# adaLN attention + ternary FFN block on one core: the reciprocal rms is spread through DRAM, and the input is scaled in the next step's layer norm stretch

## What is computed

```python
xn  = rms_norm(x, g_norm) * (1.0 + scale) + shift        # scale, shift: cond @ W_emb + b_emb, one row per sequence
q, k, v = split(xn @ W_qkv);  q, k = rms_norm(q), rms_norm(k)
o   = softmax(q @ k.T * d**-0.5) @ v;  y = o + o @ W_out
h   = gelu(bitlinear(y, w_fc));  x = x + bitlinear(h, w_proj)   # bitlinear: layer_norm, absmax quant, ternary weights
rms_norm(x, g) = x * rsqrt(mean(x * x) + 1e-6) * g
```

## Time and profile before

| what | us |
|---|---|
| median of 3 runs | 1168.1 (1166.49 to 1168.19) |
| profiled execution, its own time | 1165.45 |
| its span, first to last instruction | 1163.6 |
| PE busy / DVE busy / ACT busy / POOL busy | 1075.8 / 895.6 / 814.5 / 543.1 |
| length of a step in the loop, from one `cur_s` (L1151) to the next | 65.95 |
| start of step 0, 1, 2 by the same instruction | 48.76, 122.32, 193.06 |

### The profile page before, as it was taken

The page is one execution under the profiler, slowest core; times in us unless marked ns, Lnnn a source line. Parts: engine busy times, 40 slices in busy tenths (PEclk is TensorE's granted clock), DMA queues, the critical chain, the costliest instruction groups (busy, mean ns, idle before and its releaser), DMA issues.

```text
span 1163.6 us, 26244 instructions
## 1 busy us (share of the span) xinstructions
PE 1075.8 (92%) x9484; PEld 675.8 (58%) x9484; DVE 895.6 (77%) x1616; ACT 814.5 (70%) x1372; POOL 543.1 (47%) x365
## 2 busy tenths in 40 slices
PE   5646899999999999999999999999999999999797
PEld 1324565666666565666666565666666566666463
DVE  4668768888788888878787888878787888877544
ACT  4866575867768586877768586876868586775752
POOL 1522173643718173553718174463808264462425
PEclk8868899999999999999999999999999999999889
DMA  9810303112130313112031212112131212002101
GB/s 341 302 28 1 92 20 74 56 36 57 38 90 36 72 54 72 54 25 66 36 90 36 72 54 54 55 33 75 36 90 36 72 54 45 29 25 50 38 1 55
DMA packets 75501, 74.20 MB, mean 64 GB/s; under 512 B 6592, under 2 KB 56000, under 8 KB 74944
## 3 DMA queue, kind: packets, MB, share of 16 engines
q1 hardware_dynamic: 75456, 73.59, 21.7%
HBM read 39.89 MB, written 8.39 MB: 41 GB/s over the span
## 4 chain that ended last, share of the span: by engine, by line
PE 74%; DVE 11%; ACT 9%; issue 3%; DMA 1%; SPq 0%; DVEq 0%; ACTq 0%; POOL 0%
PE F L625 10%; PE F L627 10%; PE F L782 5%; PE F L783 5%; PE QA L593 3%; PE QA L594 3%; PE QA L595 3%; PE QB L593 3%; PE QB L594 3%; PE QB L595 3%; DVE rowmax L1088 2%; PE T L813 2%; PE SA L681 2%; DVE xn_lo L1075 2%; PE SB L681 2%
## 5 line engine op out<-in xcount | busy, mean ns | idle before, releaser
L552 POOL TENSOR_TENSOR rqk<-ssq,half 128x16 f32<-128x16 f32 x64 | 186.8, 2920 | 93.6 <-DVE ssq L1241 93.4
L782 PE MATMUL F<-yT_hi,fc_t 128*128 128x256 f16 x1024 | 227.7, 274 | 0.0
L783 PE MATMUL F<-yT_lo,fc_t 128*128 128x256 f16 x1024 | 227.3, 273 | 0.0
L625 PE MATMUL F<-proj_t,hs 128*128 128x512 f16 x512 | 196.6, 384 | 3.8 <-DVE hs L1206 3.8
L627 PE MATMUL F<-proj_t,hs 128*128 128x512 f16 x512 | 196.1, 383 | 0.0
L1206 DVE SCALAR_TENSOR_TENSOR hs<-hg,g_inv,hs 128x512 f16<-128x512 f32 x128 | 142.3, 1112 | 46.4 <-ACT hs L922 44.5
L520 POOL TENSOR_TENSOR acc<-acc,hg 128x512 f32<-128x512 f32 x96 | 148.0, 1542 | 8.6
L527 POOL TENSOR_TENSOR acc<-acc,hq 128x512 f32<-128x512 f32 x96 | 123.1, 1282 | 18.4 <-ACT hq L978 8.1
L917 ACT ACTIVATE hg<-F,g_fc 128x512 f32<-128x512 f32 x128 | 87.5, 684 | 52.9 <-PE F L783 51.3
L514 POOL TENSOR_TENSOR rs<-var,half 128x1 f32<-128x1 f32 x32 | 17.6, 550 | 226.4 <-DVE var L1099 226.4
L1220 DVE TENSOR_TENSOR p_lo<-SA,p_hi 128x512 f16<-128x512 f32 x128 | 88.0, 687 | 42.0 <-ACT p_hi L938 41.8
(11 more groups left out here) (192 smaller groups left out, 2753.0 us busy)
## 6 DMA issues: line engine op xcount, KB each, us to landing
stk<-qkT SPq DMA_DIRECT2D x128, 128.0 KB, 2.5
xtok<-in_x SPq DMA_DIRECT2D x16, 512.0 KB, 3.6
xT_sb<-in_xT SPq DMA_DIRECT2D x16, 512.0 KB, 3.4
stk<-qkT SPq DMA_DIRECT2D x128, 64.0 KB, 2.1
xres<-in_x SPq DMA_DIRECT2D x16, 512.0 KB, 3.6
out<-xres SPq DMA_DIRECT2D x16, 512.0 KB, 2.8
stk<-in_w_emb SPq DMA_DIRECT2D x4, 512.0 KB, 5.5
fc_t<-in_w_qkv SPq DMA_DIRECT2D x2, 1024.0 KB, 12.1
```

The source lines that it names most:

```text
L552: pool.tensor_tensor(rqk[:, n % 2, :], ssq[:, n % 2, :], half[:, :], ALU.pow).then_inc(rqk_r, 1)
L625: pe.matmul(FB[t][:, :], hs[:, 0, k // 2, col:col + P], proj_t[:, k, :], start=(k == 0), stop=False)
L782: pe.matmul(dst, w, yT_hi[:, k, :], start=(k == 0), stop=False)
L783: mm = pe.matmul(dst, w, yT_lo[:, k, :], start=False, stop=(k == KT - 1))
```

## The change

The transpose-like spread through TensorE and bank T is kept for sequence 0 alone. For sequences 1 to 15, SyncE stores `rx` (128x2) to a DRAM row `rx_row` and reads it back into all 128 partitions as `rx_all` (128x256), where a token's number stands at position 2p + t, so VectorE reads it with a step of two elements. The four multiplications of a sequence leave head 8 of the `pre` step and stand in the step after: two (`U_EARLY`) ahead of row maximum 0 and two between `norm_bias(ffn, 1)` and row maximum 4. In step 0, which has no `ffn`, all four stand ahead of row maximum 0. ScalarE makes `xn_hi` of the first two parts at the step's start and of the other two after the second `yT_hi` (L896). SyncE's two new transfers stand between `xres` and the first `stk<-qkT`.

```diff
@@ SyncE
+                if pre is not None and not first(pre):
+                    sp.wait_ge(rx_r, nth(pre, 1, 1))
+                    if not first(pre - 1):
+                        sp.wait_ge(ld_all, nth(pre, 16, -16))
+                    sp.dma_start(rx_row, rx[:, :]).then_inc(ld_row, 16)
+                    wait_scaled(sp, pre - 1, KT)
+                    sp.wait_ge(ld_row, nth(pre, 16, 0))
+                    sp.dma_start(rx_all[:, :], rx_row.rearrange("p t -> (p t)").partition_broadcast(P)).then_inc(ld_all, 16)
                 if qkv is not None:
                     sp.wait_ge(unturned, turn(i, ("piece", 3)) + 1)
@@ TensorE, at head 8
-                    if kind == "rms" and pre is not None:
+                    if kind == "rms" and pre is not None and first(pre):
@@ ScalarE
-                    act.wait_ge(unturned, turn(i - 1, ("rms", 0)) + 1)
-                    for k in range(KT):
-                        act.activation(xn_hi[:, k, :], u[:, k, :], ACT.Identity, bias=cur_s[:, k:k + 1]
-                                       ).then_inc(xhi_r, 1)
+                    input_hi(qkv, range(0, KT if ffn is None else U_EARLY))
...
+                if qkv is not None and ffn is not None:
+                    input_hi(qkv, range(U_EARLY, KT))
                 if pre is not None:
                     act.wait_ge(ld_xtok, nth(pre, 16, 16))
@@ VectorE
+            def scaled(b, ks):
+                by_t = rx_all[:, :].rearrange("q (p t) -> q t p", t=TT)
+                dve.wait_ge(ld_all, nth(b, 16, 0))
+                dve.wait_ge(ld_xT, nth(b, 16, 16))
+                for k in ks:
+                    dve.scalar_tensor_tensor(u[:, k, :].rearrange("q (t p) -> q t p", t=TT),
+                                             xT_sb[:, k, :].rearrange("q (t p) -> q t p", t=TT), cur_a[:, k:k + 1],
+                                             by_t, ALU.mult, ALU.mult).then_inc(u_r, 1)
...
+                if qkv is not None and not first(qkv):
+                    wait_scaled(dve, qkv - 1, KT)
+                    gains(qkv)
+                    dve.wait_ge(cur_a_r, nth(qkv, 1, 1))
+                    scaled(qkv, range(0, KT if ffn is None else U_EARLY))
...
                 if ffn is not None:
                     norm_bias(ffn, 1)
+                    if qkv is not None:
+                        scaled(qkv, range(U_EARLY, KT))
                 maxes((4, 5))
```

More of the change, by code:

```diff
@@ L49 @@
 INPUT_LOW_UNIT = 1
+U_EARLY = 2
 BEHIND = 2
@@ L151, in turn_uses @@
     runs = {"y": ffn, "stats": ffn, "max": att, "heads": att, "piece": qkv, "rms": pre}
+    if not (isinstance(i, int) and i == -2):
+        runs["rms"] = None
     uses = [("y", 0), ("y", 1), ("max", 0)] + [turn_at(i)[slot] for slot in sorted(turn_at(i))] + [("heads", 3)]
@@ L225, in adaln_ffn_kernel @@
         rx = sb("rx", [P, TT])
+        rx_row = nc.dram_tensor("rx_row", (P, TT), F32).ap()
+        rx_all = sb("rx_all", [P, N])
         xn_hi = sb("xn_hi", [P, KT, N], F16)
@@ L295, in adaln_ffn_kernel @@
         ld_xres = sem("ld_xres")
+        ld_row = sem("ld_row")
+        ld_all = sem("ld_all")
         dma_m = sem("dma_m")
@@ L396, in run, with wait_scaled @@
             iteration(B + 1)
+        def wait_scaled(engine, b, k):
+            if first(b):
+                engine.wait_ge(unturned, turn(-2, ("rms", 0)) + 1)
+            else:
+                engine.wait_ge(u_r, nth(b, KT, k) - 1)
         def piece_bank(b, n):
@@ L471, in iteration @@
                             sp.dma_start(stk[0:DH, dst, w, :], qkT[src, :, HI_Q + w, :]).then_inc(dma_stk[j], 16)
-                        for c, first in ((1, LO_Q), (2, HI_Q)):
-                            sp.dma_start(stk[DH * c:DH * c + DH, dst, :, :], qkT[src, :, first:first + 3:2, :]
+                        for c, lead in ((1, LO_Q), (2, HI_Q)):
+                            sp.dma_start(stk[DH * c:DH * c + DH, dst, :, :], qkT[src, :, lead:lead + 3:2, :]
                                          ).then_inc(dma_stk[j], 16)
@@ L864, in rounded, with input_hi @@
                                scale=inv[:, w:w + 1]).then_inc(s_round, 1)
+            def input_hi(b, ks):
+                for k in ks:
+                    wait_scaled(act, b, k + 1)
+                    act.activation(xn_hi[:, k, :], u[:, k, :], ACT.Identity, bias=cur_s[:, k:k + 1]).then_inc(xhi_r, 1)
             def iteration(i):
@@ L1144, in residual, with gains @@
                                          ALU.mult, ALU.add).then_inc(out_r, 1)
+            def gains(b):
+                dve.tensor_scalar(cur_a[:, :], mod_a[:, :, bass.ds(b, 1)].rearrange("p k o -> p (k o)"),
+                                  XQ_SCALE, None, ALU.mult).then_inc(cur_a_r, 1)
+            def scaled(b, ks):
+                by_t = rx_all[:, :].rearrange("q (p t) -> q t p", t=TT)
+                dve.wait_ge(ld_all, nth(b, 16, 0))
+                dve.wait_ge(ld_xT, nth(b, 16, 16))
+                for k in ks:
+                    dve.scalar_tensor_tensor(u[:, k, :].rearrange("q (t p) -> q t p", t=TT),
+                                             xT_sb[:, k, :].rearrange("q (t p) -> q t p", t=TT), cur_a[:, k:k + 1],
+                                             by_t, ALU.mult, ALU.mult).then_inc(u_r, 1)
             def iteration(i):
@@ L1152, in iteration @@
                                       XQ_SCALE, None, ALU.mult).then_inc(cur_s_r, 1)
[L1153 to L1157, removed]
+                if pre is not None and first(pre):
+                    gains(pre)
+                if qkv is not None and not first(qkv):
[3 more added lines that the diff above has]
+                    scaled(qkv, range(0, KT if ffn is None else U_EARLY))
                 def maxes(ks):
```

## The result

| | before | changed |
|---|---|---|
| median of 15 runs, us | 1166.87 (1164.74 to 1168.29) | 1171.97 (1168.64 to 1173.72) |
| profiled execution, us | 1165.45 | 1173.29 |
| length of a step in the loop, us | 65.95 | 65.98 |
| start of step 0, 1, 2, 3 by `cur_s`, us | 48.76, 122.32, 193.06, 259.09 | 47.55, 126.88, 198.74, 264.42 |

The ratio is 1.0043, with a 95% interval of 1.0035 to 1.0051. Forecast was +3.85 us with 1167.5 to 1178.0 as the range. The last row locates the loss. It is there by the start of step 3 (264.42 against 259.09, +5.3), and from there to step 14 it grows by only 0.3.

A forecast was written before the change was run, and what follows sets the result against it. The prediction took TensorE's issue and waits to bound the loop, and ScalarE's chain step 0. Terms of 2.5 (step 0), 0.65 (loop) and 0.7 (step 14) made +3.85 on 1168.1: 1171.9 us, range 1167.5 to 1178.0.

The forecast's parts named there:

- The loop: Each of 13 loop steps: 0.72 us added in layer norm less 0.67 saved on TensorE, +0.05 a step, +0.65 in all.
- Regained at head 8: Attention, head 8: without the spread, scores follow PV at once, and TensorE keeps all 0.67 us a step.
- The pairs: Layer norm stretch: the moved multiplications delay row maximum 4, and so `y_turn(1)` and all behind it, by 0.72 us.
- the first pair: Two multiplications ahead of row maximum 0: shift that maximum by 0.67 us and the statistics and second bias by 0.50.
- The second pair: Two multiplications behind the second bias: take 0.78 us, use up 0.51 idle, row maximum 4 shifted by 0.72.
- Step 0: VectorE waits for `rx_all` behind the weights; ScalarE's `xn_hi` is 3.0 us later, less 0.53 for the spread: +2.5.
- Step 14: The step without `pre`: pays the layer norm shift of 0.72 us and saves nothing, counted as +0.7.
- Hidden landing: Rival, step 0: the store passes the weights, `rx_all` there by 49.0; sum +1.4, 1169.5 us, no change; chance 0.13.
- The idle time swallows the first pair: Rival, layer norm stretch: only the later two multiplications count, shift 0.22, -0.45 a step, 1165.0 us; chance 0.06.
- Half rate: Rival, moved multiplications: the step of two elements halves VectorE's rate, +1.13 a step, 1187 us; chance 0.06.
- Not regained: Rival, attention: GpSimd or the T bank holds it, TensorE's 0.67 us is lost; +12.6, 1180.7 us; chance 0.06.

The follow-up runs named there:

- Experiment 3: Changed kernel without the transfers: TensorE spreads at head 8 every step, VectorE copies the row to `rx_all`, multiplications stay moved; 1176.36 us, ratio 1.0076 to the kernel before.
- Experiment 6: Changed kernel with sequences 0 and 1 spread by TensorE, second multiplications behind row maximum 7, their `xn_hi` behind the Gelu table load; 1161.71 us, ratio 0.9955.
- experiments 1: Changed kernel, but sequences 0 and 1 spread by TensorE and scaled in attention as before; transfers serve sequences 2 to 15; 1165.4 us, ratio 0.9987.
- experiment 2: Changed kernel, but in step -1 ScalarE instead of SyncE issues the store and read-back of sequence 1; 1167.01 us, ratio 0.9994.
- experiment 4: Changed kernel with sequences 0 and 1 spread by TensorE and multiplications back in attention, three at head 12, one at head 13; 1167.06 us, ratio 0.9996.

## Why the prediction was right, and where it was not

The median came 0.1 us from the forecast. That is luck: the two terms of the loop were off and met, and the whole sum was short by what the starting median was too high. The chain of waits in step 0 and the balance in the loop were right.

- **The loop (+0.05 a step forecast, +0.03 measured): right, with both terms too large.** Regained at head 8: 0.67 forecast and 0.67 found, but 0.12 is lost again at the third piece's transposes, so 0.55 stays. The prediction had looked for what is late next only at the last piece and only at GpSimd, where it found 0.9 us to spare; the wait came one piece earlier, at bank T, for VectorE's `oT_lo`. The pairs: 0.72 forecast, 0.57 found in the changed kernel. Experiment 3, where nothing is regained, has them at 0.67. There `y_turn(1)` stands just as far behind `cur_s` (+0.57), but TensorE's first matmul of the step comes 0.10 earlier against `cur_s`. So what the pairs cost depends also on where TensorE stands against VectorE when the step begins, and the two terms aren't quite independent.
- **Inside the pairs' term** the single starts were right (0.40 from `cur_a` forecast, 0.41 measured; 0.78 a pair, 0.79 measured), but the first pair was mis-sized: I let its delay at the second bias, 0.50, run through to `y_turn(1)`. Experiment 6 shows 0.13 of it there. What `y_turn(1)` needs is row maximum 4, and that waits, where no second pair stands in front, not for VectorE's row but for TensorE's maxima (the 0.28 idle in experiment 6, the 0.51 in the earlier trace rows), which came only 0.13 late. The second pair was the dear one, 0.44. Their sum hid this.
- **Step 0 (+2.5 forecast): the mechanism right, the size short.** Step 1 starts 4.6 us later. The chain was as forecast: the store behind the input rows, the read-back behind the store, VectorE waiting, ScalarE handing the delay on. Three links were longer: the input rows took 14.1 us instead of 12.7 (landed 49.9 instead of 48.6), the store landed 0.6 behind them instead of 0.4, and the read-back took 4.3 instead of the 2.4 that I had taken from `stk<-qkT`. That one moves data out of SBUF, this one spreads a DRAM row over all partitions; which of these differences makes the price, no run shows. Together 54.9 instead of 51.4 for the first multiplication: 3.5 of the 3.6 us by which `xn_hi` (+6.58) exceeds the forecast +3.0. The giving back was larger too, 2.0 by step 1's start against 0.53; how much of it is the spread and VectorE's 1.57 and how much the clock, isn't settled.
- **Steps 1 and 2** add 1.1 and give back 0.35 in the changed kernel's trace. In the loop's form they do what later steps do, and the half-clock stretches of steps 0 and 1 fall elsewhere (before: 129.2 to 136.0 us; after: 133.9 to 144.2, among others). I ascribe the difference to that, but no run shows it.
- **Step 14 (+0.7)** can't be seen. The time from step 14's start (the last `cur_s`) to the end is 179.0 us before and 181.3 after, but 178.9, 180.3 and 179.3 in experiments 1, 2 and 6, which have the same tail as the changed kernel. The tail scatters by more than the term.
- **Why then the median to 0.1 us?** The forecast started from 1168.1, and the median of the kernel before was 1166.9 in the later runs. By difference it is +5.1 measured against +3.85: short by 1.25, and the start was 1.23 too high.

The rivals. *Hidden landing* needed the store to pass the weights. On SyncE's queue it did not; on ScalarE's queue it did, and experiment 2 gave 1167.0 where the rival had 1169.5. *The idle time swallows the first pair* was nearer the truth than its 0.06 says: 0.13 left of that pair. It missed the time since its other half, the second pair at 0.22, was wrong. *Half rate*: four multiplications with a step of two in `rx_all` take 1.67 us, as those without did, and in experiment 3, which reads the same row without the step, one follows another at 0.40 us as here. *Not regained* is what experiment 4 shows for another placement.

The rule of the Trainium skill's page "DMA: Bandwidth & Descriptors" (Rules for kernel authors), issue early and wait late, held for the loop, where the two transfers of 2.9 and 3.9 us cost nothing. In step -1 the issue wasn't early: `rx` was ready at 30.1 us and SyncE came to it at 37.94, with 4.5 MB of bulk transfers ahead. By that rule the price would have been the hidden landing's 1.4 us; the medians have 5.1.

## What to carry to other kernels

A small transfer on the path goes on a queue that holds no bulk transfer, and is issued by an engine whose list comes to it in time: one kilobyte behind five bulk transfers took 12.5 us and was issued 7.8 us after its data was ready; on another queue it was issued 6.2 us earlier and took 7.5, and the choice was worth the whole loss of this change. Moving work between stretches is a sum of two prices, what its absence gives back and what its presence takes, and both are set by the row of idle times around the place: the same four multiplications cost 0.57 us, 0.13 us, all of the gain, or nothing, in four placements. After a removal, look for what is late next at every wait of the stretch, not at the one that looks tightest.

## What the runs showed of the hardware

- In the changed kernel's trace a store of 1 KB to DRAM takes 2.6 to 4.2 us in steps 0 to 13 (median 2.9), and a read-back of 128 KB, one DRAM row into all 128 partitions, 2.9 to 4.1 us (median 3.9). The DMA engines are busy some 0.2 of the time in the loop. The 128 KB `stk<-qkT` took 2.5 before the change.
- With the DMA engines full (the weights in step -1), the same small store took 7.5 us on a queue of its own, and the read-back 6.8; the store landed 7.9 us before a 1 MB transfer that another queue had been given 1.6 us earlier. Behind five bulk transfers on the same queue the store took 12.5 us.
- An issue to a queue with bulk transfers ahead held SyncE 3.24 us instead of 0.34; at such a time ScalarE's, to the empty queue, took 0.35.
- An fp32 multiplication on VectorE of which one operand in SBUF has an inner step of two elements takes what a contiguous one takes: 1.67 us for four of 128x256, 0.40 us from one to the next with the step and without it (experiment 3).
